# Second mixture of a four-layer graph network: all experts for all nodes beside the attention's edge loop, in place of routing, sorted rows and an expert stage of their own

## The reference

```python
h = (x_flat @ W_gat).reshape(M, HEADS, NUM_EXPERTS)                 # 4 heads, 4 experts
...                                                                # attention over 131072 edges and a loop per node
agg = jax.ops.segment_sum(msg, dst, num_segments=M).reshape(M, HEADS * NUM_EXPERTS) + b_gat
scores = _layernorm(agg, ln_gamma, ln_beta).reshape(M, HEADS, NUM_EXPERTS).mean(1)
topk_s, topk_i = jax.lax.top_k(scores, TOP_K)                       # 2 of 4
w = jax.nn.softmax(topk_s, axis=-1)
out = jnp.zeros_like(x)
for ei in range(NUM_EXPERTS):
    g = jnp.where(topk_i == ei, w, 0.0).sum(-1)
    hh = jax.nn.gelu(x @ W1[ei] + b1[ei], approximate=False)        # 256 -> 512
    out = out + g[..., None] * (hh @ W2[ei] + b2[ei])               # 512 -> 256
```

## Time and profile before

| | |
|---|---|
| time, median of 3 runs | 9246.27 us (9236.26 to 9251.24) |
| the profiled execution | 9241.27 us, span 9239.5 us |
| PE / DVE / POOL / ACT busy, share of the span | 64% / 59% / 58% / 33% |
| mean granted clock of PE | 0.772 of 2.4 GHz |

### The profile page before, as it was taken

One profiled execution on the slowest core, in us unless ns is written; L12 is line 12 of the kernel. 1 busy time (PEld: TensorE's weight loads), 2 busy tenths in 40 slices (PEclk: granted clock), 3 DMA queues, 4 the chain that ended last, 5 costly groups with the idle time before them and its releaser, 6 DMA issues. The chain is left out here.

```text
span 9239.5 us, 116147 instructions
## 1 busy us (share of the span) xinstructions
PE 5910.0 (64%) x27490; PEld 4485.2 (49%) x27491; DVE 5467.6 (59%) x14668; ACT 3028.1 (33%) x8882; POOL 5321.7 (58%) x5289
## 2 busy tenths in 40 slices
PE   1366777772398655565566666197567776484499
PEld 0133555552377333444455555186445554363387
DVE  8787888886574766655333333322667776535544
ACT  0123888884322200002222222322244443412322
POOL 0362666664655577773777777466377772542422
PEclk9688999995599877776555555599788898596599
DMA  9413656652265333331000001175533334374355
GB/s 302 136 52 104 175 168 175 174 172 75 90 208 176 120 101 101 102 102 37 9 8 8 8 8 8 65 215 182 183 104 104 104 104 105 128 227 108 104 196 166
DMA packets 685645, 1088.08 MB, mean 118 GB/s; under 512 B 139599, under 2 KB 473511, under 8 KB 684892
## 3 DMA queue, kind: packets, MB, share of 16 engines
q0 software_dynamic: 248352, 553.07, 21.9%
q1 hardware_dynamic: 411052, 476.40, 16.6%
q10 hardware_dynamic: 25744, 53.10, 2.0%
HBM read 864.19 MB, written 226.64 MB: 118 GB/s over the span
## 5 line engine op out<-in xcount | busy, mean ns | idle before, releaser
L3886 POOL DMA_INDIRECT gat_edges_rows<-gat_table,gat_room x1080 | 1108.7, 1027 | 449.7 <-issue 328.8
L2527 POOL DMA_INDIRECT l_edges_ring<-pairs,first_room x832 | 842.2, 1012 | 592.3 <-issue 242.8
L2089 POOL DMA_INDIRECT l_sum_rows<-l_feats,back_room x832 | 826.6, 994 | 321.9 <-issue 241.3
L2109 PE MATMUL l_sum_o<-l_sum_rows,l_sum_s 128*128 128x256 f32 x1664 | 609.6, 527 | 450.6 <-DVE l_sum_s L2120 242.6
L2578 ACT ACTIVATE l_edges_ring<-l_edges_ring,l_edges_weight 128x64 f32<-128x64 f32 x3328 | 816.6, 336 | 0.0
L3657 PE MATMUL m_ffn_yp<-m_ffn_w2b,m_ffn_ht 128*128 128x256 f32 x3200 | 740.0, 384 | 46.9 <-ACT m_ffn_ht L3679 46.0
L3679 ACT ACTIVATE m_ffn_ht<-m_ffn_hp,m_ffn_b1t 128x256 f32<-128x256 f32 x800 | 378.6, 474 | 1182.0 <-PE m_ffn_hp L3647 1181.6
L3647 PE MATMUL m_ffn_hp<-m_ffn_xt,m_ffn_w1b 128*128 128x256 f32 x3200 | 738.7, 384 | 7.1 <-DVE m_ffn_xt L3694 4.4
L2109 PEld LDWEIGHTS l_sum_o<-l_sum_rows,l_sum_s 128*128 128x128 f32 x1664 | 413.0, 262 | 641.3 <-DVE l_sum_s L2120 310.9
L3657 PEld LDWEIGHTS m_ffn_yp<-m_ffn_w2b,m_ffn_ht 128*128 128x128 f32 x3200 | 592.7, 190 | 157.4 <-ACT m_ffn_ht L3679 43.7
L3647 PEld LDWEIGHTS m_ffn_hp<-m_ffn_xt,m_ffn_w1b 128*128 128x128 f32 x3200 | 606.1, 192 | 108.7 <-ACT m_ffn_ht L3679 15.9
(11 more groups left out here) (896 smaller groups left out, 14255.8 us busy)
## 6 DMA issues: line engine op xcount, KB each, us to landing
m_ffn_w1b<-in_L_ffn_W SPq DMA_DIRECT2D x108, 512.0 KB, 4.5
m_ffn_w2b<-in_L_ffn_W SPq DMA_DIRECT2D x108, 512.0 KB
sorted_rows<-count_main_zero ACTq DMA_DIRECT2D x1, 51858.0 KB, 237.4
m_ffn_xs<-sorted_rows SPq DMA_DIRECT2D x196, 258.0 KB, 3.3
m_ffn_w1b<-in_L_ffn_w SPq DMA_DIRECT2D x32, 1024.0 KB, 6.3
m_ffn_w2b<-in_L_ffn_w SPq DMA_DIRECT2D x32, 1024.0 KB, 5.4
l_proj_taken<-m_by_node SPq DMA_DIRECT2D x42, 768.0 KB, 6.7
m_ffn_b2b<-in_L_ffn_b SPq DMA_DIRECT2D x196, 128.0 KB, 3.5
```

The costliest lines, as they stand in the source:

```text
L2089: pool.indirect_dma_start(rows[:, slot, j, :], None, table, bass.IndirectOffsetOnAxis(ap=L.src[:, t:t + 1], axis=0)).then_inc(got[slot], 16)
L2109: pe.matmul(o[:, j, 0:D], s4[:, q % S4, j, :], rows[:, slot, j, :], start=True, stop=True).then_inc(out_done, 1)
L2527: pool.indirect_dma_start(rows(q, 0, 2 * D)[:, j, :], None, table, bass.IndirectOffsetOnAxis(ap=L.src[:, t:t + 1], axis=0)).then_inc(got[q ...
L3886: pool.indirect_dma_start(rows[:, slot, j, :], None, table, bass.IndirectOffsetOnAxis(ap=L.src[:, q * B + j:q * B + j + 1], axis=0)).then_ ...
```

## The change

The expert stage and the routing of the second mixture are gone. In their place:

- `gat_project` keeps its transposed tiles (`keep_zt`, in the buffer `l_acc` that the front has just read), and carries 14 quads of record moves.
- `gat_edges` gets `DenseExperts`: each of the four experts is applied to all nodes, in 25 runs of up to two tiles each. PE's and ACT's queues get its instructions in 404 ticks, about one after each third of a quad's work; SP loads the weights and stores the results as rows by node, four for each node.
- In the loop, ACT's `widen` is gone. DVE makes the float32 one-hots itself (`wide`), and the bfloat16 ones have 3 buffers and not 12. The sums in PSUM are laid out in three banks and not four, to make room. The loop is written out in full, not as a hardware loop of 12 quads.
- `gat_scores` also picks the two best experts and makes a weight for each of the four (zero for two of them).
- The front of `l2_proj` is `DenseFront`: four rows are loaded and added for each node.
- `MOVES` is `(3, 6, 58, 8, 5, 16, 54, 22, 14, 10)`: of the 50 quads that rode in the removed stage, 13 go to the first projection, 1 and 14 to the first mixture's projection and experts, 8 to the second layer's projection and 14 to `gat_project`.

```diff
-MOVES = (3, 6, 45, 8, 5, 15, 40, 14, 50, 10)
+MOVES = (3, 6, 58, 8, 5, 16, 54, 22, 14, 10)
...
+class DenseFront(Front):
...
+    def load(self, sp, c):
+        if c >= 2:
+            sp.wait_ge(self.added[-1], (c - 1) * CH)
+        for k in range(self.E):
...
+    def work(self, dve):
+        def adder(k):
+            def add(t, par):
...
+                dve.scalar_tensor_tensor(out=x, in0=self.rows[0:n, c % 2, k, j, :], scalar=self.weight[0:n, t, k:k + 1],
+                                         in1=x, op0=ALU.mult, op1=ALU.add).then_inc(self.added[k], 1)
...
+class DenseExperts:
...
+    def share(self, ticks, slot):
+        whole = self.SLOTS * self.n
+
+        def some(q, _):
+            at = self.SLOTS * q + slot
+            for _ in range((at + 1) * self.ticks // whole - at * self.ticks // whole):
+                next(ticks, None)
+        return some
...
+    def tensor(self, pe):
+        def up(q, i):
+            e, t, n = self.of(q)
+            pe.wait_ge(self.w1_in, 16 * (e + 1))
+            if q or i:
+                pe.wait_ge(self.ht_ready, 4 * q + 2 * i)
+            for j in range(2):
+                k = 2 * i + j
+                for c in range(DC):
+                    ins = pe.matmul(self.hp[:, j, 0:n * P], self.w1b[:, c, k * P:(k + 1) * P],
+                                    self.zt[:, t:t + n, c * P:(c + 1) * P], start=(c == 0), stop=(c == DC - 1))
+            ins.then_inc(self.h_done, 1)
+
+        def down(q, h):
...
+            pe.wait_ge(self.ht_ready, 4 * (q + 1))
...
+            if q:
+                pe.wait_ge(self.y_ready, q)
+            pe.matmul(self.yp[:, h, :], self.core.ident[0:self.E, e:e + 1].to_broadcast([self.E, P]), self.b2r[:], start=True,
+                      stop=False)
+            for k in range(self.HC):
+                ins = pe.matmul(self.yp[:, h, :], self.ht[:, q % 2, k, h * P:(h + 1) * P], self.w2b[:, k, :],
+                                start=False, stop=(k == self.HC - 1))
...
+        for q in range(self.runs + 1):
+            for i in range(2):
+                if q < self.runs:
+                    up(q, i)
+                yield
+                if q:
+                    down(q - 1, i)
+                yield
+
+    def scalar(self, act):
+        def activate(q, i):
...
+            for j in range(2):
+                k = 2 * i + j
+                act.activation(self.ht[:, q % 2, k, 0:n * P], self.hp[:, j, 0:n * P], ACT.Gelu,
+                               bias=self.b1t[:, e * self.HC + k:e * self.HC + k + 1]).then_inc(self.ht_ready, 1)
...
-                def widen(q, slot):
-                    act.wait_ge(s_ready, q + 1)
-                    if past(q, CK):
-                        act.wait_ge(out_done, (q - CK + 1) * B)
-                    act.copy(sf[:, slot % CK], s8[:, slot]).then_inc(sf_ready, 1)
-                steps(act, n, [(1, copy_st), (9, widen), (2, repeat), (6, expo), (3, spread)], **whole)
+                dense.biases_in(act)
+                ticks = dense.scalar(act)
+                steps(act, n, [(1, copy_st), (0, dense.share(ticks, 0)), (2, repeat), (0, dense.share(ticks, 1)),
+                               (6, expo), (3, spread), (0, dense.share(ticks, 2))], **whole)
...
-                steps(pe, n, [(2, fetch), (1, turn_s), (10, collect), (6, lower), (5, reach_back), (4, meet), (3, flip)],
-                      **whole)
+                ticks = dense.tensor(pe)
+                steps(pe, n, [(2, fetch), (1, turn_s), (0, dense.share(ticks, 0)), (10, collect), (0, dense.share(ticks, 1)),
+                              (6, lower), (5, reach_back), (4, meet), (3, flip), (0, dense.share(ticks, 2))], **whole)
...
+                def wide(q, slot):
+                    if q >= CK:
+                        dve.wait_ge(out_done, (q - CK + 1) * B)
+                    dve.tensor_tensor(sf[:, slot % CK], bc(core.row[:], 1, [P, B, P]),
+                                      bc(L.dst[:, ds(q * B, B)], 2, [P, B, P]), ALU.is_equal).then_inc(sf_ready, 1)
...
-        RouteFollow(R, G.scores, None, core.sorted_rows, top=True).alone(nc, core, "m1_put")
-        experts(nc, core, R, core.sorted_rows, by_node, w["W1"], w["b1"], w["W2"], w["b2"], ACT.Gelu,
-                unmoved.take(MOVES[8]))
-        return TakeFront(R, by_node)
```

More of the change, by code:

```diff
@@ L2915, in __init__ @@
         self.nmean = sb("nmean", [P, T])
-        self.weight = [sb(f"weight{k}", [P, T, 2]) for k in range(4)]
+        four = sb("weight12", [P, T, 4])
+        self.weight = [sb("weight0", [P, T, 2]), four, four, sb("weight3", [P, T, 2])]
         self.ends = sb("ends_of_firsts", [P, 2, T], I32)
@@ L3822, in gat_edges @@
+def gat_edges(nc, core, L, table, acc, ma, slope, zt, w, by_node, spare, numbers):
     H, W, B, CK, U, NW = 4, 16, 8, 3, 12, 6
@@ L3854, in gat_edges @@
         az = cuts[:, 0:2 * RW].rearrange("o (k r) -> o k r", k=2)
-        sums4 = ph.ps("sums", [P, 4, 512])
-        sums = sums4[:].rearrange("p k c -> p (k c)").rearrange("p (t r) -> p t r", r=SLOT)
+        column = numbers[0:1, 0:TE].bitcast(I32)
+        sums4 = ph.ps("sums", [P, BK, 512])
+        assert BK * SB >= T and SB * SLOT <= 512 and R <= SLOT
+        sums = sums4[:].rearrange("p k c -> p (k c)")
         stp = ph.ps("stp", [P, B, P], BF16)
@@ L3875, in gat_edges, with columns_of, _ @@
         opened = lambda q, slot: q - slot % CK
+        def columns_of(engine, q):
+            _, vals = nc.values_load_multi_w_load_instructions(column[0:1, ds(q * B, B)], engines=(engine,), min_val=0,
+                                                               max_val=(T - 1) * SLOT + 2 * (BK - 1),
+                                                               skip_runtime_bounds_check_because="made from blocks below T")
+            return vals
         with nc.Block() as block:
+            @block.sync
+            def _(sp):
+                dense.sync(sp)
             @block.gpsimd
@@ L4028, in _ @@
                 dve.wait_ge(lasts, BK)
-                ol = Own(dve, linked, 12).at(0)
+                ol = Own(dve, linked, 15).at(0)
+                past_bank, past_both = from_last[:, 0:TE], to_last[:, 0:TE]
+                ol.mark(dve.tensor_scalar(past_bank, blocks, float(SB), 2.0, ALU.is_ge, ALU.mult))
+                ol.then(dve.tensor_scalar(past_both, blocks, float(2 * SB), 2.0, ALU.is_ge, ALU.mult))
+                ol.then(dve.tensor_tensor(past_bank, past_bank, past_both, ALU.add))
+                ol.then(dve.scalar_tensor_tensor(out=column, in0=blocks, scalar=float(SLOT), in1=past_bank,
+                                                 op0=ALU.mult, op1=ALU.add))
                 for k in range(BK):
@@ L4211, in _, with gat_scores @@
                 act.activation(flat(ex[:]), flat(ex[:]), ACT.Exp).then_inc(done, 1)
-def gat_scores(nc, core, acc, scores, w):
+def gat_scores(nc, core, acc, scores, w, weight):
     H, C = 4, 4
@@ L4227, in gat_scores @@
         own, loaded, rooted = ph.sem("own"), ph.sem("loaded"), ph.sem("rooted")
+        left = ph.sb("left", [P, T, H])
+        apart = ph.sb("apart", [P, T, H])
+        first = ph.sb("first", [P, T])
+        best = ph.sb("best", [P, 2, T])
+        share = ph.sb("share", [P, 2, T])
+        chosen = ph.sb("chosen", [P, 2, T, H])
+        diff = ph.sb("diff", [P, T])
+        diff_ready, diff_exp = ph.sem("diff_ready"), ph.sem("diff_exp")
         with nc.Block() as block:
@@ L4283, in __init__, with gat_project @@
         self.table = nc.dram_tensor("gat_table", [T * P, 20], F32).ap()
-def gat_project(nc, core, G, w, front):
+def gat_project(nc, core, G, w, front, zt, beside):
     HE = 16
@@ L4393, in gnn_stack_kernel @@
                             nc, ph, core, const, gat, ei[1], ei[0], True, 1, 1))
[L4394 to L4395 removed]
+                        gat_project(nc, core, G, w[3], front, acc, unmoved.take(MOVES[8]))
+                        front = layer1_ffn(nc, core, G, gat, w[3], acc, back, const.slot)
         with ExitStack() as c2:
```

228 lines of the change are left out of this document (186 added, 42 removed).

## The result

The kernel after the change takes 8799.5 us (median of 4 runs, 8796.1 to 8805.2), the kernel before 9241.3 beside it: ratio 0.952, 95% interval 0.951 to 0.954. The profiled execution has a span of 8803.1 us.

A forecast was written before the change was run, and what follows sets the result against it. The prediction took POOL's gathers to bound the edge loop and PE the expert stage. From 9241 us, 9241 - 588 + 95 + 13 + 55 + 15 = 8831 us; it named 8830, range 8720 to 9080.

The forecast's parts named there:

- the likeliest case: Whole kernel: PE paces the edge loop at nearly full clock; 8830 us, own range 8760 to 8930, chance 0.55.
- signs of being wrong: Edge loop and moves: PE idle behind ACT, clock below 0.9, gathers well over 1.03 us, or move-taking stages growing by tens.
- Routing and experts, -588: Second mixture's routing (148 us) and expert stage (440 us): whole stages between barriers, so all 588 us leave the path.
- Edge loop, +95 predicted: Edge loop with the experts added: PE needs 1533 us for what took 1438, +95 us, ends +0 and +203.
- They almost tie: Edge loop: PE's content of 1352 us at full clock set against POOL's 1438 us.
- POOL keeps the pace: Rival, chance 0.15: edge loop stays at 1438 us plus part of 0 to 90 us; 8736 us without them.
- The drain: Edge loop, ACT: about 1.38 us more per table load, adding 62 us to PE's waits; left out of the sum.
- The exclusive lock: Edge loop, port pair of DVE and GpSimd: new one-hots could hold gathers 165 us in total, loop 70 us longer.
- Scores, +13: `gat_scores`: 21 short DVE operations with a wait each, 0.6 us apiece, all on the path, +13 us.
- Next projection, +55, ends 35 and 75: Next projection, four more rows a node: larger of DVE adds (46 us) and bytes (52 us), with longer fill, +55 us.
- Record moves, +15: Stages taking over record moves: mostly hidden at about 1.3 us of POOL each, together +15 us, 0 to 60.
- The two rivals with a slower clock: Edge loop: PE's clock comes only halfway (chance 0.22, 9050 us) or stays at 1.2 GHz (chance 0.06, 9747 us).

The follow-up runs named there:

- f2: Kernel after the change, writing only one of eight tiles of each new float32 one-hot from the fourth quad on; 8795 us, ratio 0.951 to the kernel before.
- f3: Kernel after the change, with the next projection fetching experts' rows tile by tile, ten tiles ahead, between the stores; 8759 us, ratio 0.947 to the kernel before.
- e6: Kernel before the change, with only its `MOVES` line replaced by the one of after; 9248 us, ratio 0.9993 to the kernel before.
- c1: Kernel after the change, unchanged, profiled on a slower chip; 10774 us, ratio 0.984 to the kernel before there.
- c2: Kernel before the change, unchanged, profiled on a slower chip; 10946 us.
- f1: Kernel after the change, leaving out three of four hidden blocks of each expert's second product; 8794 us, ratio 0.951 to the kernel before.

## Why the prediction was right, and where it was not

8831 us was summed and 8805 came, inside the likeliest case's own range. That it came so near is in part luck: the likeliest case had PE pace the loop, and POOL does; and the terms are off by -30, -5, +22 and -15 us, which partly cancel. Two of the prediction's own signs of being wrong came true, a clock below 0.9 in the loop (0.89) and gathers well over 1.03 us (1.085). Term by term:

- **Routing and experts, -588:** as predicted.
- **Edge loop, +95 predicted, +65 measured.** The mis-sized step is the subtraction, of PE's content less what the gathers filled. PE's content was priced at 1533 us, and f2, where PE paces, has 1525 from barrier to barrier: right to 8 us. But that content covers the whole stage, the 39 us behind the last gather too, where PE goes on working. It had to stand against the stage's 1477 us, not against the gathers' 1438; that gives +56, and the +65 that came are POOL's, by its longer gathers. Inside the 1533, errors cancelled, so the 8 us are luck as well: `fetch`, left whole at 146 us, fell to 51; the bias products, priced at 85 us (392 of 0.216), took 143; the clock was 0.89 and not 0.94; the wait at `flip` grew by 60 us and not by 35. `collect` was read from a window that ends at 5812 us, with 2123 of its 2160 products; the whole stage has all 2160, 486 us and not 478, which moves the sum by some 4 us.
- **Which engine paces:** the likeliest case said PE, with gathers no longer back to back. That sign is absent. PE's limit (1525) lies 12 us under POOL's 1537.5, because the new one-hots lengthened the gathers by 58 ns in the mean, 63 us in sum. "They almost tie" was said of other numbers, 1352 us of PE at full clock against 1438. The longer gathers were counted at nothing, since POOL would have 95 us to spare; it had none. Of the 0 to 90 us given for them, two thirds were paid. The rival *POOL keeps the pace*, given 0.15, named the mechanism: 8736 plus a part of those 90, with 63 us 8799.
- **ACT, 530 us with 86 table loads:** 519 with 86. The drain that the Trainium skill's page "ScalarE: Activation LUTs" (section "What ACT_TABLE_LOAD costs") adds to a load is not there: the 43 loads ahead of `expo` start 0.02 us after the GELU before them, and the exponential starts 0.01 us after the load. In the one wait shown above, `flip` waits through the 1.28 us of the load and the end of a GELU ahead of it; over the loop it waits 2.2 us a time against 0.8.
- **The exclusive lock** of the Trainium skill's page "SBUF — State Buffer" (section "SBUF: two separate sides"): the page calls the port pair that VectorE and GpSimd share an exclusive lock, held for a whole instruction. By it the prediction let the new one-hots hold the gathers for up to 165 us. The sum grew by 63, 0.46 us for each of 135; f2 took 0.054 x 1080 = 58 us of it back. Single gathers agree with the page all the same, but for the 0.01 to 0.02 us by which those held by a pair start first. In the trace of before 127 of them start while a one-hot runs, and each ends 0.81 to 1.03 us after that one-hot does; of 109 beside which a one-hot starts later, 102 keep their 0.94 us. So a gather is held for what is left of the one-hot when it starts, and for both of a pair where it starts with the pair. What a one-hot costs hangs on where it falls.
- **Scores, +13:** +8. The 0.6 us an operation were read from a row that joins two stages.
- **Next projection, +55, ends 35 and 75:** +77, just outside the ends. The step priced DVE's adds (46) and the bytes (52) as running at once and took the larger; DVE's adds took 39 us more, and 40 us more of idle time stand before its copy. The order in one queue was not priced: a store of 128 KB behind 3.7 MB of loads, with a buffer of two results waiting for it. f3 took 43 us back.
- **Record moves, +15:** next to nothing here (e6, and +2 us in `gat_project`), 181 us on the chip of c1 and c2, of which the 60 us of the upper end would have held a third.
- **The two rivals with a slower clock** did not come: in stretches of 100 to 200 us from 4400 to 5860 us the loop's clock was 0.85 to 0.97.

## What to carry to other kernels

When a second engine's work is put beside a paced loop, compare its whole content with the whole stage, and price what the new work does to the pacing engine's own instructions before counting it as hidden. Two limits that lie close hide each other: lifting either alone gave 1%, both 4% of the loop, so test them in pairs. A bulk load ahead of small stores in one queue stops whoever waits for the stores; issue it in pieces between them.

## What the runs showed that was not expected

- **Less work for PE, and a lower clock.** f1 has 254 us less work for PE than after, yet its busy time fell by only 63 us (1399 to 1335). The granted clock fell from 0.89 to 0.75, and an up product of 256 columns took 518 ns in the mean and not 405. What lowers the clock there no run shows.
- **Register instructions can hide behind array work.** `fetch`, 1080 small products with a register's address each, kept PE busy for 146 us before and for 51 us once products of 256 columns stood ahead of it. The clock rose from 0.50 to 0.89 as well, but half of 146 would still be 73. That the sequencer does the register's work while the array is busy is how I read it; no run separated it.
- **Chips differ by 17 to 18% on the same kernel,** and the change is worth 4.8% on one kind and 1.6% on the other. On the second kind more goes (routing and experts, 835 us and not 588), but the loop grows by 422 us and not by 65, and the moves cost 181 us and not nothing.
